# Attention core with 256-token chunks: one chunk of each half worked as two single 128-token tiles

## The chip, the cores and the metric

One core of one Trainium2 chip runs the whole program. The metric is the device time of one execution in microseconds. The kernel before takes 2043.13 us, the median of three runs.

## The reference, cut to what matters

The input is 8 sequences of 1024 tokens with 256 features, fp32. A mixture-of-experts layer, an attention-like layer and a second expert layer follow each other. The change lies in the attention-like layer:

```python
n = _ln(x, ln_g, ln_b)
W1 = _mlp(n, h1_w1, h1_b1, h1_w2, h1_b2)
W2 = _mlp(n, h2_w1, h2_b1, h2_w2, h2_b2)
W3 = jnp.einsum('bzn,bsn->bzs', W1, W2)
W3 = jnp.tril(W3)
t = jnp.einsum('bzs,bsm->bzm', W3, n)
t = _ln(_gelu(t), ln_g, ln_b)
x1 = x + t
out = x + _mlp(_ln(x1, ln_g, ln_b), fm_w1, fm_b1, fm_w2, fm_b2)
```

There is no softmax between the scores and t. So for a token z, the tokens s that lie in earlier blocks can be summed up first: their part of t is W1[z] times the state, the sum of W2[s]^T n[s] over those blocks. Only the scores inside z's own block have to be formed and masked.

## The kernel before, in words

**Tiling.** The 8192 tokens are worked in 16 halves of 512 tokens, two for each sequence. A half is even (j = 0, 2, ...) where it begins a sequence and odd where it ends one. A tile is 128 tokens, a half has four tiles and two chunks of 256 tokens (c = 0 and 1).

**Order.** The order on each engine is written out by hand as positions. A half j > 0 has 24 positions: 8 for each of the three multi-layer networks h1, h2 (of this half) and fm (of the half before). At each position TensorE issues `up` (six matmuls of 512 columns, L2133), then `down` for the position two earlier (L2163 or L2153), and then, at some positions, a piece of the attention core. ScalarE (ACT) makes two gelus of each `up` result (L1430, L1433), VectorE (DVE) subtracts one from the other (`rest`, L1815) so that `down` can work in a high and a low part.

**The core of half j.** Position 18: scores (`score_tiles`, L2209), for each chunk a block of 128 rows of W2 by 256 columns and one of 128 by 128; ACT copies them out (L1465) and GpSimd (POOL) masks the diagonal blocks (L1348). Position 19: W2 is turned (`turn_w2`, L2217) and copied (L1846). Position 20: the state of each chunk (`state_tiles`, L2226), which DVE copies or adds to the one before (`add_state`, L1857 and L1860). Position 21: t (`t_tiles`): scores times n (L2242), and, where there are tokens in earlier chunks, W1 times the state (L2246); ACT takes the gelu of t into `t_rows` (L1470). Position 22: the next half's n is turned (`turn`, L2121). Half 0 has the same pieces in a row at its end, with nothing between them.

**Banks.** All these pieces write the two PSUM banks `work0` and `work1` in turn; who reads a bank must be done before the next piece writes it. `t_rows` is free from position 13, where TensorE has turned it, to position 21, where the gelu of t is written. Each fp32 matmul of the program stands in the trace as two matmul rows; those of the networks, in the rounded form fp32r, as one.

**The queues.** SyncE's and POOL's DMAs are not touched by the change. POOL, in order: roots, gathers and scatters for the neighbouring expert layers, the mask, and three sums over rows (L1336 to L1341) that wait for DVE's L1773.

Of the kernel before, what the change touches and what calls it, by code (L numbers as in the profile page):

```python
# [16 lines left out]
ALU = mybir.AluOpType  # L17
# [859 lines left out]
def attention_to_end(nc, outer, tag, consts, routing, home, w, base_d, y_d, base1_d, xs_d, meta_d, y2_d, out):  # L877
# [21 lines left out]
    TURN_M, TURN_N, SCORES, W2_ROWS, STATE, T_SUM, TURN_X, LOGITS, PLACES = range(9)  # L899
# [8 lines left out]
    for j in range(HALVES + 2):  # L908
# [13 lines left out]
        if j < HALVES:  # L922
            take_work(j, SCORES)
            take_work(j, W2_ROWS, (0, 1) if j % 2 == 0 else (0,))
            take_work(j, STATE, (0, 1) if j % 2 == 0 else (0,))
            take_work(j, T_SUM)
# [3 lines left out]
    def work_use(bank, j, what):  # L930
        return uses[bank, j, what]

    with ExitStack() as ctx:
# [7 lines left out]
        gelu = [sb(f"gelu{s}", [P, GW]) for s in range(GELUS)]  # L941
        hid_pair = [sb(f"hid{s}", [P, 2, GW], fr) for s in range(PARTS)]
        hid = [[pair[:, part, :] for part in range(2)] for pair in hid_pair]
        over_hid = [nc.alloc_sbuf_tensor_at(f"final_total{11 + s}", [P, GT, D], fp32, offset=nc.sbuf_base - 2 * 4 * 2 * GW + s * 4 * 2 * GW) for s in range(2)]
        proj = room[:, 4096:6144].rearrange("p (m k n) -> p m k n", m=2, k=KD)
# [108 lines left out]

        def z_of(j):
            return zn[:, j % 2, 0, :, :]
# [4 lines left out]
        def state_of(j, chunk):  # L1061

            return state[(2 * (j % 2) + chunk) % 2]
# [49 lines left out]
        for j in range(HALVES):  # L1113
            state_count.append(state_count[-1] + (2 if j % 2 == 0 else 1))

        def w2_count(j):

            return state_count[j]
# [131 lines left out]
        def _(pool):  # L1250
# [92 lines left out]
            def mask(j):  # L1343
                for c in range(2):
                    pool.wait_ge(scores_out, 2 * j + c + 1)
                    for lo in (0, CW):
# [69 lines left out]
        def _(act):  # L1416
# [42 lines left out]
            def copy_scores(j):  # L1459
# [174 lines left out]
        def _(dve):  # L1634
# [213 lines left out]
            def add_state(j):  # L1848
                for c in range(2 - j % 2):
                    dve.wait_ge(work_full[c], work_use(c, j, STATE) + 1)  # L1850
                    if j:

                        for bank in range(2):
                            dve.wait_ge(work_full[bank], work_use(bank, j - 1, T_SUM) + 1)
                    dst, src = state_of(j, c), work[c][:, :].rearrange("p (k d) -> p k d", k=KD)
                    if j % 2 == 0 and c == 0:
                        dve.tensor_copy(dst[:, :, :], src).then_inc(state_ready, 1)  # L1857
                    else:
                        dve.wait_ge(state_ready, state_count[j] + c)
                        dve.tensor_tensor(dst[:, :, :], src, state_of(j, c - 1)[:, :, :], ALU.add).then_inc(state_ready, 1)  # L1860

            def iteration(j):
                more, h = j + 1 < HALVES, j - 2
                for pos in range(PER if j else 2 * FC):
# [46 lines left out]
                    if j == 0 and pos == 15:  # L1911
# [3 lines left out]
                        add_state(0)  # L1915
# [4 lines left out]
                    if pos == 20:  # L1920
                        add_state(j)
# [190 lines left out]
        def _(pe):  # L2112
            TERMS = ((0, 0), (1, 0), (0, 1))

            def turn(src, emptied, count):

                for k in range(KD):
                    if emptied is not None:
                        pe.wait_ge(emptied, count + k + 1)
# [100 lines left out]
            def state_tiles(j):  # L2220

                for c in range(2 - j % 2):
                    pe.wait_ge(w2_ready, w2_count(j) + c + 1)
                    for k in range(KD):
                        for s in range(2):
                            last = pe.matmul(work[c][:, k * D:(k + 1) * D], w2_rows[:, 2 * c + s, k * P:(k + 1) * P], n_of(j)[:, 2 * c + s, :], start=(s == 0), stop=(s == 1))  # L2226
                    last.then_inc(work_full[c], 1)

            def t_tiles(j):

                for c in range(2):
                    before = j % 2 or c
                    if j % 2 == 0 or c == 0:

                        pe.wait_ge(state_ready, state_count[j] + c + 1)
                    else:
                        pe.wait_ge(state_ready, state_count[j] + 1)
                    pe.wait_ge(masked, 4 * j + 2 * c + 2)
                    for d in range(2):
                        out = work[c][:, d * D:(d + 1) * D]  # L2240
                        for s in range(d + 1):
                            last = pe.matmul(out, scores[:, c, d * P:(d + 1) * P] if s == 0 else scores[:, c, CW:CW + P], n_of(j)[:, 2 * c + s, :],  # L2242
                                             start=(s == 0), stop=(s == d and not before))
                        if before:
                            for k in range(KD):
                                last = pe.matmul(out, proj[:, 0, k, (2 * c + d) * P:(2 * c + d + 1) * P], state_of(j, c - 1)[:, k, :], start=False, stop=(k == KD - 1))  # L2246
                    last.then_inc(work_full[c], 1)

            def iteration(j):
                positions = PER if j else 2 * FC  # L2250
                for pos in range(positions):
# [9 lines left out]
                    if j:  # L2261
# [4 lines left out]
                        if pos == 13:  # L2266
                            pe.wait_ge(t_step, 16 * j)
                            if j == 1:
                                turn(t_rows, t_gelu, 0)
# [9 lines left out]
                        if pos == 20:  # L2279
                            state_tiles(j)  # L2280
                        if pos == 21:
                            t_tiles(j)
# [245 lines left out]
```

## Time and profile before

| | |
|---|---|
| three runs, median (lowest to highest) | 2043.13 us (2042.89 to 2043.6) |
| profiled execution, first to last instruction (its only time shown) | 2040.7 us |
| TensorE busy | 1945.9 us, 95% of the span |
| VectorE, ScalarE, GpSimd busy | 1305.8, 1093.1, 1102.2 us |
| mean granted TensorE clock | 0.982 of full speed |
| attention halves 0 to 15, from about 396 to 1684 us of the span | positions as above |

The profiled execution's span is 2.4 us under the median of the runs; what lies around it (start and end of the program) is in the runs only. A row of the timeline is the start in us, the duration, the engine, the line, the operation and how many instructions are merged in it; the duration of a merged row goes from its first start to its last end. Matmuls overlap, so a row's duration is longer than the step from one to the next.

### The profile page before, as it was taken

To read this page: it belongs to the slowest core of one execution; us is meant where nothing else is said; L and a number is where in the kernel's file an instruction comes from. 1 tells how busy PE (TensorE), PEld (TensorE's weight loads), DVE (VectorE), ACT (ScalarE), POOL (GpSimd) and SP (SyncE) were. 2 spreads that over 40 slices of the span, in tenths; PEclk is the share of its full clock that TensorE was granted. 3 is DMA by queue.
4 is the path that set the end of the run, shared out by engine and by line. 5 is a ranking of instruction groups with operands and counts; after the bars stand their busy time and mean duration, and the time that the engine had idled before them with its cause. 6 is when DMAs were issued, how large, how long until landed. Compare 5 with 4: busy or idle time off the path is not lost.

```text
span 2040.7 us, 32594 instructions
## 1 busy us (share of the span) xinstructions
PE 1945.9 (95%) x11074; PEld 1661.1 (81%) x11074; DVE 1305.8 (64%) x3481; ACT 1093.1 (54%) x1988; POOL 1102.2 (54%) x1262
## 2 busy tenths in 40 slices
PE   6997999699999999999999999999999996899998
PEld 4776999578888888888888888888888886599975
DVE  5996677456557576575665765756657545466659
ACT  6873777334545455454454544544545534577775
POOL 5664777442364555645546456455552532577753
PEclk9998999899999999999999999999999998899998
DMA  8544999790022032120320311102100040499969
GB/s 278 183 158 135 323 325 323 227 278 22 13 92 83 22 104 60 45 88 16 104 83 22 104 29 34 42 21 62 42 22 24 19 132 9 93 343 328 397 234 333
DMA packets 234295, 267.99 MB, mean 131 GB/s; under 512 B 25425, under 2 KB 184210, under 8 KB 234130
## 3 DMA queue, kind: packets, MB, share of 16 engines
q1 hardware_dynamic: 205458, 198.69, 29.9%
q0 software_dynamic: 28672, 67.22, 9.7%
q8 instruction: 89, 1.46, 0.3%
q14 instruction: 76, 0.62, 0.1%
HBM read 149.31 MB, written 116.52 MB: 130 GB/s over the span
## 4 chain that ended last, share of the span: by engine, by line
PE 67%; DVE 8%; issue 3%; ACT 2%; POOL 1%; DMA 1%; DVEq 0%; SPq 0%; ACTq 0%; POOLq 0%
PE attention_ring L2133 23%; PE attention_acc L2163 14%; PE attention_acc L2153 9%; PE attention_acc L2403 3%; PE attention_ring L2391 2%; PE attention_acc L2391 2%; PE attention_work L2209 2%; DVE attention_hid L1815 2%; PE attention_work L2226 2%; PE attention_work L2242 2%; PE attention_work L2246 2%; PE attention_ring L2378 1%; PE attention_work L2121 1%; PE attention_work L2183 1%; ACT attention_xn L1443 1%
## 5 line engine op out<-in xcount | busy, mean ns | idle before, releaser
L1815 DVE TENSOR_TENSOR attention_hid<-attention_gelu,attention_hid 128x512 fp32r<-128x512 f32 x384 | 286.7, 747 | 487.7 <-ACT attention_gelu L1433 318.2
L1430 ACT ACTIVATE attention_hid<-attention_ring,home_b 128x512 fp32r<-128x512 f32 x384 | 264.3, 688 | 533.7 <-PE attention_ring L2133 533.2
L2163 PE MATMUL attention_acc<-attention_hid,home_w_h 128*128 128x512 f32 x1024 | 361.2, 391 | 3.1 <-DVE home_room L1832 1.7
L1433 ACT ACTIVATE attention_gelu<-attention_ring,home_b 128x512 f32<-128x512 f32 x384 | 261.6, 681 | 0.0
L2163 PEld LDWEIGHTS attention_acc<-attention_hid,home_w_h 128*128 128x128 f32 x1024 | 192.2, 188 | 49.3 <-DVE home_room L1832 9.4
L2133 PE MATMUL attention_ring<-attention_n_t_h,home_w_h 128*128 128x512 f32 x512 | 203.9, 398 | 1.6 <-DVE attention_n_t_l L1807 1.6
L2153 PE MATMUL attention_acc<-home_w_h,attention_hid 128*128 128x256 f32 x1024 | 204.4, 283 | 0.0
L2133 PE MATMUL attention_ring<-attention_n_t_h,home_w_l 128*128 128x512 f32 x512 | 199.8, 390 | 0.0
L2133 PE MATMUL attention_ring<-attention_n_t_l,home_w_h 128*128 128x512 f32 x512 | 199.5, 390 | 0.0
L2163 PE MATMUL attention_acc<-attention_hid,home_w_l 128*128 128x512 f32 x512 | 199.3, 389 | 0.0
L1260 POOL DMA_INDIRECT home_room<-expert_rows,routing_slots x128 | 136.5, 1066 | 91.6 <-DVE home_room L1646 38.1
L1314 POOL DMA_INDIRECT slot_rows<-attention_xn,attention_slot_at x120 | 123.6, 1030 | 94.7 <-DVE attention_meta_at L1750 62.8
L2153 PEld LDWEIGHTS attention_acc<-home_w_h,attention_hid 128*128 128x128 f32 x1024 | 167.6, 190 | 5.0
L684 POOL DMA_INDIRECT early_xg<-xn_rows,routing_affine x124 | 136.1, 1098 | 40.8 <-issue 39.9
L1325 POOL DMA_INDIRECT slot_ids<-attention_row_id,attention_meta_at x128 | 127.4, 995 | 36.9 <-issue 36.9
L2153 PE MATMUL attention_acc<-home_w_l,attention_hid 128*128 128x256 f32 x512 | 144.6, 282 | 0.0
L2133 PE MATMUL attention_ring<-attention_m_t_h,home_w_h 128*128 128x512 f32 x256 | 112.5, 440 | 1.4 <-DVE attention_m_t_l L1807 1.4
L2133 PEld LDWEIGHTS attention_ring<-attention_n_t_l,home_w_h 128*128 128x128 f32 x512 | 96.1, 188 | 20.7
L2163 PEld LDWEIGHTS attention_acc<-attention_hid,home_w_l 128*128 128x128 f32 x512 | 96.1, 188 | 19.5
L2133 PEld LDWEIGHTS attention_ring<-attention_n_t_h,home_w_h 128*128 128x128 f32 x512 | 96.4, 188 | 19.0 <-DVE attention_n_t_l L1807 1.8
L2133 PEld LDWEIGHTS attention_ring<-attention_n_t_h,home_w_l 128*128 128x128 f32 x512 | 96.5, 188 | 16.9
L2133 PE MATMUL attention_ring<-attention_m_t_l,home_w_h 128*128 128x512 f32 x256 | 101.4, 396 | 0.0
(330 smaller groups left out, 4819.3 us busy)
## 6 DMA issues: line engine op xcount, KB each, us to landing
early_w<-in_L_ffn_w SPq DMA_DIRECT2D x64, 256.0 KB, 4.7
expert_rows<-experts_y SPq DMA_DIRECT2D x64, 256.0 KB, 4.0
slot_rows<-const_zeros SPq DMA_DIRECT2D x16, 1024.0 KB, 10.3
token_rows<-const_zeros SPq DMA_DIRECT2D x16, 1024.0 KB, 10.0
home_room<-in_L_ffn_w SPq DMA_DIRECT2D x64, 256.0 KB, 4.8
final_y_rows<-token_rows SPq DMA_DIRECT2D x32, 512.0 KB, 7.7
dispatch_x_in<-in_L_attn_x SPq DMA_DIRECT2D x16, 512.0 KB, 6.7
xn_rows<-dispatch_xn SPq DMA_DIRECT2D x16, 512.0 KB, 4.2
```

What stands on the lines that cost most here:

```text
L684: pool.indirect_dma_start(out=xg[e % R][:, c, :], out_offset=None, in_=xn_d, in_offset=bass.IndirectOffsetOnAxis(ap=routing["lists"][:, e, ...
L1260: pool.indirect_dma_start(out=ye[:, t, k, :], out_offset=None, in_=y_d, in_offset=bass.IndirectOffsetOnAxis(ap=routing["slots"][:, j * GT ...
L1314: pool.indirect_dma_start(out=xs_d, out_offset=bass.IndirectOffsetOnAxis(ap=slot_at[h % 2][:, k, t:t + 1], axis=0), in_=xn_of(h)[:, t, :], ...
L1325: pool.indirect_dma_start(out=meta_d, out_offset=bass.IndirectOffsetOnAxis(ap=meta_at[h % 2][:, k, t:t + 1], axis=0), in_=row_id[h % 2][:, ...
L1430: act.activation(hid[n % PARTS][0][:, :], ring[n % RING][:, :], ACT.Gelu, bias=b1[:, m, c:c + 1])
L1433: act.activation(gelu[n % GELUS][:, :], ring[n % RING][:, :], ACT.Gelu, bias=b1[:, m, c:c + 1]).then_inc(ring_free, 1)
L1815: dve.tensor_tensor(hid[n % PARTS][1][:, :], gelu[n % GELUS][:, :], hid[n % PARTS][0][:, :].bitcast(fp32), ALU.subtract).then_inc(hid_read ...
L2133: last = pe.matmul(ring[n % RING][:, :], w1[m][wp][:, k, c * P:(c + 1) * P], rows_t[xp][:, k, :], start=(q == 0), stop=(q == 2 * len(TERMS ...
L2153: last = pe.matmul(acc[e % 3][:, (t % 2) * D:(t % 2 + 1) * D], hid[s][xp][:, t * P:(t + 1) * P], w2[m][wp][:, c, :], start=(c == 0 and q = ...
L2163: last = pe.matmul(acc[e % 3][:, :], w2[m][wp][:, c, k * P:(k + 1) * P], hid[s][xp][:, :], start=(c == 0 and q == 0), stop=(c == FC - 1 an ...
L2391: last = pe.matmul(ps_gu[e % EF][:, half, :], wt[e % EF][:, k, half * INNER:(half + 1) * INNER], xt[e % EX][:, k, :], start=(n == 0), stop ...
L2403: last = pe.matmul(ps_y[e % EF][:, c, :], e_hidden[e % EF][:, c * P:(c + 1) * P], e_w2[e % WR], start=True, stop=True)
```

## The change

In each half one chunk stays as it was: chunk 0 in even halves, chunk 1 in odd ones (`joined`). The other is worked as two single tiles. For it only the two 128x128 diagonal blocks of the scores are formed, and its second tile takes what precedes it from a state that includes its first tile. So an even half has three states (after tiles 0 and 1, after tile 2, after tile 3) and an odd half forms two new ones (after tile 0, after tile 1). The additional state buffers lie in `t_rows`. In even halves t is formed for chunk 1 first and then for chunk 0, because bank 0 holds the third state until DVE has added it; the gelus of t and the turning at position 22 follow that order. Two buffers, `gelu` and `hid`, change places in SBUF.

```diff
-    TURN_M, TURN_N, SCORES, W2_ROWS, STATE, T_SUM, TURN_X, LOGITS, PLACES = range(9)
+    TURN_M, TURN_N, SCORES, W2_ROWS, STATE, THIRD_STATE, T_SUM, TURN_X, LOGITS, PLACES = range(10)
...
+    def joined(j, pair):
+
+        return pair == j % 2
+
+    def score_blocks(j, pair):
+
+        return ((0, CW, 0), (CW, P, 1)) if joined(j, pair) else ((0, P, 0), (P, P, 1))
...
+        def t_order(j):
+
+            return (1, 0) if j % 2 == 0 else (0, 1)
...
+        early_state, late_state = [t_rows[:, 2 * c:2 * c + 2, :] for c in range(2)]
+
+        def state_after(j, n):
+
+            if j % 2 == 0:
+                return (early_state, state[0], state[1])[n]
+            return (state[0], late_state, state[1])[n]
...
-                    act.activation(scores[:, c, :], work[c][:, 0:CW + P], ACT.Copy).then_inc(scores_out, 1)
+                    wide = CW + P if joined(j, c) else CW
+                    act.activation(scores[:, c, 0:wide], work[c][:, 0:wide], ACT.Copy).then_inc(scores_out, 1)
...
-                for c in range(2):
+                for c in t_order(j):
...
+            def add_state(j, n):
+
+                bank, what = (0, THIRD_STATE) if n == 2 else (n, STATE)
+                dve.wait_ge(work_full[bank], work_use(bank, j, what) + 1)
...
+                dst, src = state_after(j, n), work[bank][:, :].rearrange("p (k d) -> p k d", k=KD)
+                if j % 2 == 0 and n == 0:
+                    dve.tensor_copy(dst[:, :, :], src).then_inc(state_ready, 1)
+                else:
+                    dve.wait_ge(state_ready, state_count[j] + n)
+                    dve.tensor_tensor(dst[:, :, :], src, state_after(j, n - 1)[:, :, :], ALU.add).then_inc(state_ready, 1)
...
                     if pos == 20:
-                        add_state(j)
+                        add_state(j, 0)
+                        add_state(j, 1)
+                    if pos == 21 and j % 2 == 0:
+                        add_state(j, 2)
...
-                    for lo, width, s in ((0, CW, 2 * c), (CW, P, 2 * c + 1)):
+                    for lo, width, s in score_blocks(j, c):
+                        at = (2 * c + s) * P
                         for k in range(KD):
-                            last = pe.matmul(work[c][:, lo:lo + width], proj[:, 1, k, s * P:(s + 1) * P], proj[:, 0, k, 2 * (c + 1) * P - width:2 * (c + 1) * P], start=(k == 0), stop=(k == KD - 1))
+                            last = pe.matmul(work[c][:, lo:lo + width], proj[:, 1, k, at:at + P], proj[:, 0, k, at:at + width], start=(k == 0), stop=(k == KD - 1))
...
+            def state_tiles(j, n):
+
+                if j % 2 == 0:
+                    bank, tiles, copied = ((0, (0, 1), 1), (1, (2,), 2), (0, (3,), 2))[n]
+                else:
+                    bank, tiles, copied = ((0, (0,), 1), (1, (1,), 1))[n]
+                pe.wait_ge(w2_ready, w2_count(j) + copied)
+                if n == 2:
+                    pe.wait_ge(state_ready, state_count[j] + 1)
+                if j % 2 and n == 1:
+                    pe.wait_ge(scores_out, 2 * j + 2)
+                for k in range(KD):
+                    for s in tiles:
+                        last = pe.matmul(work[bank][:, k * D:(k + 1) * D], w2_rows[:, s, k * P:(k + 1) * P], n_of(j)[:, s, :], start=(s == tiles[0]), stop=(s == tiles[-1]))
+                last.then_inc(work_full[bank], 1)
...
+                    if j % 2 == 0:
+                        pe.wait_ge(state_ready, state_count[j] + (2 if c else 3))
+                    else:
                         pe.wait_ge(state_ready, state_count[j] + c + 1)
...
+                        t, out = 2 * c + d, work[c][:, d * D:(d + 1) * D]
+                        if joined(j, c):
+                            seen = None if j % 2 == 0 else state_after(j, 1)
+                            parts = [(scores[:, c, d * P:(d + 1) * P], 2 * c)] + ([(scores[:, c, CW:CW + P], 2 * c + 1)] if d else [])
+                        else:
+                            seen = state_after(j, d) if c else state_after(j, d - 1)
+                            parts = [(scores[:, c, d * P:(d + 1) * P], t)]
...
                         if pos == 20:
-                            state_tiles(j)
+                            state_tiles(j, 0)
+                            state_tiles(j, 1)
                         if pos == 21:
+                            if j % 2 == 0:
+                                state_tiles(j, 2)
                             t_tiles(j)
                         if pos == 22 and j + 1 < HALVES:
                             pe.wait_ge(n_ready, 8 * (j + 2))
-                            turn(n_of(j + 1), t_gelu, 2 * j)
+                            turn(n_of(j + 1), t_gelu, 2 * j, t_order(j))
```

How this stands on the engines. TensorE, half 2 (an even one), position 18, the scores. Before:

```order
L2153 MATMUL attention_acc<-home_w_2_h,attention_hid 128x256
L2209 MATMUL attention_work<-home_room 128x256 x2
L2209 MATMUL attention_work<-home_room 128x128 x2
L2209 MATMUL attention_work<-home_room 128x256 x2
L2209 MATMUL attention_work<-home_room 128x128 x2
L2133 MATMUL attention_ring<-attention_m_t_h,home_w_2_h 128x512
```

Now:

```order
L2177 MATMUL attention_acc<-home_w_2_l,attention_hid 128x256
L2177 MATMUL attention_acc<-home_w_2_h,attention_hid 128x256
L2234 MATMUL attention_work<-home_room 128x256 x2
L2234 MATMUL attention_work<-home_room 128x128 x6
L2157 MATMUL attention_ring<-attention_m_t_h,home_w_2_h 128x512
```

Two matmuls of 256 columns have become two of 128; nothing else has moved there.

TensorE, half 2, position 21: the t block (L2242 scores times n, L2246 W1 times a state; now L2278 and L2281). Before:

```order
L2153 MATMUL attention_acc<-home_w_2_h,attention_hid 128x256
L2242 MATMUL attention_work<-home_room,attention_scores 128x256 x4
L2246 MATMUL attention_work<-attention_state,home_room 128x256 x2
L2242 MATMUL attention_work<-home_room,attention_scores 128x256 x2
L2246 MATMUL attention_work<-attention_state,home_room 128x256 x2
L2133 MATMUL attention_ring<-attention_m_t_h,home_w_2_h 128x512
```

Now, where L2258 is the third state's matmuls:

```order
L2177 MATMUL attention_acc<-home_w_2_h,attention_hid 128x256
L2258 MATMUL attention_work<-home_room,attention_w_rows 128x256 x2
L2278 MATMUL attention_work<-home_room,attention_scores 128x256
L2281 MATMUL attention_work<-attention_t_rows,home_room 128x256 x2
L2278 MATMUL attention_work<-home_room,attention_scores 128x256
L2281 MATMUL attention_work<-attention_state,home_room 128x256 x2
L2278 MATMUL attention_work<-home_room,attention_scores 128x256 x3
L2157 MATMUL attention_ring<-attention_m_t_h,home_w_2_h 128x512
```

Two state matmuls have come here from position 20, and the t block has nine matmuls where it had ten.

VectorE, half 2, positions 20 to 22 (`hid` is `rest`, `home_room` at L1773 the next half's n). Before:

```order
L1815 TENSOR_TENSOR attention_hid0<-attention_gelu0,attention_hid0 128x512
L1773 SCALAR_TENSOR_TENSOR home_room<-home_room,attention_x_root,home_b_row 128x256 x4
L1857 COPY attention_state0<-attention_work0 128x512
L1860 TENSOR_TENSOR attention_state1<-attention_work1,attention_state0 128x512
L1815 TENSOR_TENSOR attention_hid1<-attention_gelu1,attention_hid1 128x512
L1815 TENSOR_TENSOR attention_hid2<-attention_gelu0,attention_hid2 128x512
```

Now:

```order
L1834 TENSOR_TENSOR attention_hid0<-attention_gelu0,attention_hid0 128x512
L1792 SCALAR_TENSOR_TENSOR home_room<-home_room,attention_x_root,home_b_row 128x256 x4
L1877 COPY attention_t_rows<-attention_work0 128x512
L1880 TENSOR_TENSOR attention_state0<-attention_work1,attention_t_rows 128x512
L1834 TENSOR_TENSOR attention_hid1<-attention_gelu1,attention_hid1 128x512
L1880 TENSOR_TENSOR attention_state1<-attention_work0,attention_state0 128x512
L1834 TENSOR_TENSOR attention_hid2<-attention_gelu0,attention_hid2 128x512
```

One addition is new, between two `rest` operations; in an odd half the new one stands at position 20, right behind the first.

## Rows read from the trace of the kernel before

**Rows 1.** Busy time of each engine in one window, halves 1 to 15.

```profile
core 0: us, PE busy (x) PEld busy (x) DVE busy (x) ACT busy (x) POOL busy (x), PEclk, DMA share, GB/s
452.40:1679.20 1226.80, 1224.99 (x6544) 1053.98 (x6543) 758.94 (x2064) 585.61 (x976) 623.19 (x719) 1.00 0.17 54
```

**Rows 2.** Waits of TensorE over the span: us in total, times, longest.

```profile
PE attention_work L2121 <- DVE attention_t_rows L1802: 12.9, 1, 12.9
...
PE attention_acc L2163 <- DVE home_room L1832: 1.7, 2, 1.3
...
PE attention_ring L2133 <- DVE attention_n_t_l L1807: 1.6, 1, 1.6
```

**Rows 3.** Timeline of TensorE, half 6 (even), positions 18 to 20.

```profile
917.58 2.78 PE L2209 MATMUL attention_work<-home_room 128*128 128x256 f32 x16
920.12 0.47 PE L2133 MATMUL attention_ring<-attention_m_t_h,home_w_h 128*128 128x512 f32 x1
...
926.70 3.62 PE L2226 MATMUL attention_work<-home_room,attention_w_rows 128*128 128x256 f32 x16
929.97 0.58 PE L2133 MATMUL attention_ring<-attention_m_t_h,home_w_h 128*128 128x512 f32 x1
```

**Rows 4.** By line: durations in ns, min/median/max, first and last start, forms.

```profile
L2209 PEld LDWEIGHTS attention_work<-home_room x256: 186/190/192, 443.2 to 1662.0; 128*128 128x128 f32 x128
L2209 PE MATMUL attention_work<-home_room x256: 272/326/454, 443.3 to 1662.2; 128*128 128x256 f32 x64, 128*128 128x128 f32 x64
...
L2246 PE MATMUL attention_work<-attention_state,home_room x192: 379/379/379, 452.6 to 1678.7; 128*128 128x256 f32 x192
```

**Rows 5.** Timeline of TensorE, the router's matmuls of 64 columns at the end.

```profile
1715.83 1.90 PE L2183 MATMUL attention_work<-home_gate,attention_w_rows 128*128 128x64 f32 x16
```

**Rows 6.** Timeline of TensorE, half 6, positions 21 and 22.

```profile
932.98 1.89 PE L2242 MATMUL attention_work<-home_room,attention_scores 128*128 128x256 f32 x8
934.70 1.03 PE L2246 MATMUL attention_work<-attention_state,home_room 128*128 128x256 f32 x4
935.57 1.03 PE L2242 MATMUL attention_work<-home_room,attention_scores 128*128 128x256 f32 x4
936.43 1.03 PE L2246 MATMUL attention_work<-attention_state,home_room 128*128 128x256 f32 x4
937.11 0.58 PE L2133 MATMUL attention_ring<-attention_m_t_h,home_w_h 128*128 128x512 f32 x1
```

**Rows 7.** Timeline of VectorE, half 6, positions 20 and 21.

```profile
929.03 0.68 DVE L1857 COPY attention_state<-attention_work 128x512 f32<-128x512 f32 x1
930.35 0.69 DVE L1860 TENSOR_TENSOR attention_state<-attention_work,attention_state 128x512 f32<-128x512 f32 x1 [0.64 <-PE attention_work L2226]
933.11 0.95 DVE L1815 TENSOR_TENSOR attention_hid<-attention_gelu,attention_hid 128x512 fp32r<-128x512 f32 x1 [2.06 <-ACT attention_gelu L1433]
```

**Rows 8.** Timeline of VectorE and TensorE, half 7 (odd), positions 20 and 21.

```profile
1011.27 0.68 DVE L1860 TENSOR_TENSOR attention_state<-attention_work,attention_state 128x512 f32<-128x512 f32 x1
1013.63 1.16 DVE L1815 TENSOR_TENSOR attention_hid<-attention_gelu,attention_hid 128x512 fp32r<-128x512 f32 x1 [1.67 <-ACT attention_gelu L1433]
...
1016.52 0.59 PE L2242 MATMUL attention_work<-home_room,attention_scores 128*128 128x256 f32 x2
```

**Rows 9.** Timeline around the turning of n, end of half 6: VectorE, TensorE.

```profile
941.38 1.29 DVE L1807 TENSOR_TENSOR attention_n_t_l<-attention_work,attention_n_t_h 128x512 fp32r<-128x512 f32 x2 [0.44 <-ACT attention_n_t_h L1422]
...
943.82 0.40 PE L2133 MATMUL attention_ring<-attention_n_t_h,home_w_h 128*128 128x512 f32 x1
```

**Rows 10.** Timeline of GpSimd, from half 6 to half 7.

```profile
947.18 1.14 POOL L1325 DMA_INDIRECT slot_ids<-attention_row_id,attention_meta_at  x1 [0.30 <-issue]
949.16 0.23 POOL L1268 TENSOR_SCALAR attention_small<-attention_u_mv 128x4 f32<-128x4 f32 x1 [0.85 <-DVE attention_u_mv L1653]
```

**Rows 11.** Timeline of half 0's end: TensorE, VectorE, ScalarE's copies of the scores.

```profile
445.97 1.40 PE L2217 MATMUL attention_work<-const_eye,home_room 128*128 128x128 f32 x8
447.35 3.72 PE L2226 MATMUL attention_work<-home_room,attention_w_rows 128*128 128x256 f32 x16
...
449.38 0.69 DVE L1857 COPY attention_state<-attention_work 128x512 f32<-128x512 f32 x1 [1.29 <-PE attention_work L2226]
...
446.17 0.49 ACT L1465 ACTIVATE attention_scores<-attention_work 128x384 f32<-128x384 f32 x1 [0.82 <-PE attention_work L2209]
...
455.43 0.60 ACT L1470 ACTIVATE attention_t_rows<-attention_work 128x512 f32<-128x512 f32 x1 [2.42 <-PE attention_work L2246]
```

More of the change, by code:

```diff
@@ L944, in attention_to_end @@
         over_hid = [nc.alloc_sbuf_tensor_at(f"final_total{11 + s}", [P, GT, D], fp32, offset=nc.sbuf_base - 2 * 4 * 2 * GW + s * 4 * 2 * GW) for s in range(2)]
+        gelu = [sb(f"gelu{s}", [P, GW]) for s in range(GELUS)]
         proj = room[:, 4096:6144].rearrange("p (m k n) -> p m k n", m=2, k=KD)
@@ L1846, in copy_w2_rows @@
                     dve.tensor_copy(w2_rows[:, 2 * c:2 * c + 2, :], work[c][:, :].rearrange("p (t d) -> p t d", t=2)).then_inc(w2_ready, 1)
[L1848 to L1860, printed above, removed]
+            def add_state(j, n):
+                bank, what = (0, THIRD_STATE) if n == 2 else (n, STATE)
+                dve.wait_ge(work_full[bank], work_use(bank, j, what) + 1)
+                if j and n == 0:
+                    for c in range(2):
+                        dve.wait_ge(work_full[c], work_use(c, j - 1, T_SUM) + 1)
+                dst, src = state_after(j, n), work[bank][:, :].rearrange("p (k d) -> p k d", k=KD)
[4 more added lines that the diff above has]
+                    dve.tensor_tensor(dst[:, :, :], src, state_after(j, n - 1)[:, :, :], ALU.add).then_inc(state_ready, 1)
             def iteration(j):
@@ L1914, in iteration @@
                         copy_w2_rows(0)
-                        add_state(0)
+                        for n in range(3):
+                            add_state(0, n)
                     if pos == 17:
@@ L2113, in _, with turn @@
             TERMS = ((0, 0), (1, 0), (0, 1))
-            def turn(src, emptied, count):
-                for k in range(KD):
+            def turn(src, emptied, count, order=(0, 1)):
+                for n, k in enumerate(order):
                     if emptied is not None:
-                        pe.wait_ge(emptied, count + k + 1)
+                        pe.wait_ge(emptied, count + n + 1)
                     for t in range(GT):
@@ L2218, in turn_w2 @@
                     last.then_inc(work_full[c], 1)
[L2220 to L2227, printed above, removed]
+            def state_tiles(j, n):
[12 more added lines that the diff above has]
+                last.then_inc(work_full[bank], 1)
@@ L2238, in t_tiles @@
                     pe.wait_ge(masked, 4 * j + 2 * c + 2)
                     for d in range(2):
[L2240 to L2244, printed above, removed]
+                        t, out = 2 * c + d, work[c][:, d * D:(d + 1) * D]
@@ new lines, in t_tiles @@
+                        if joined(j, c):
[4 more added lines that the diff above has]
+                            parts = [(scores[:, c, d * P:(d + 1) * P], t)]
+                        for n, (weights, s) in enumerate(parts):
+                            last = pe.matmul(out, weights, n_of(j)[:, s, :], start=(n == 0), stop=(seen is None and n == len(parts) - 1))
@@ L2245, in t_tiles @@
+                        if seen is not None:
                             for k in range(KD):
-                                last = pe.matmul(out, proj[:, 0, k, (2 * c + d) * P:(2 * c + d + 1) * P], state_of(j, c - 1)[:, k, :], start=False, stop=(k == KD - 1))
+                                last = pe.matmul(out, proj[:, 0, k, t * P:(t + 1) * P], seen[:, k, :], start=False, stop=(k == KD - 1))
                     last.then_inc(work_full[c], 1)
@@ L2292, in iteration @@
                     turn_w2(0)
-                    state_tiles(0)
+                    for n in range(3):
+                        state_tiles(0, n)
                     t_tiles(0)
```

21 lines of the change are left out of this document (8 added, 13 removed).

## The prediction, made before the changed kernel ran

> **What bounds the kernel now.** I read the busy times by stretch first. From the end of half 0 to the t block of half 15 [rows 1] TensorE is busy for 1224.99 of 1226.80 us at a granted clock of 1.00; VectorE has 758.94, ScalarE 585.61 and GpSimd 623.19 us in the same stretch. The waits of TensorE say the same from the other side [rows 2]: over the whole span its one long wait is 12.9 us for the last t rows, behind half 15, and the others that touch this stretch are of 1.3 and 1.6 us, once each. So in the attention halves the time is the length of TensorE's stream of instructions. What shortens that stream shortens the program, as long as no other engine becomes late; what is added to VectorE costs nothing while its results come in time.
>
> **What a matmul of this core costs.** In half 6 the state's 16 matmul rows of 256 columns last 3.62 us from the first start to the last end [rows 3]. The last alone lasts 0.38, as every row of 256 columns at the neighbouring line L2246 does [rows 4], so one step is (3.62 - 0.38) / 15 = 0.216 us. The scores are 8 rows of 256 and 8 of 128 columns, 2.78 us, and the last, a narrow one, takes about 0.27 [rows 3, 4]. That leaves 2.51 us: 8 steps of 0.216 and 7 narrow ones of (2.51 - 1.73) / 7 = 0.111 us. Each fp32 matmul of the program is two such rows.
>
> **Part 1, the scores.** Two matmuls of 256 columns become two of 128, in every half: 4 rows by (0.216 - 0.111) = 0.42 us. In other cases a narrow matmul could stop getting cheaper because its weights still have to be loaded. The router's rows of 64 columns show where that floor is: 16 of them last 1.90 us [rows 5], which is (1.90 - 0.22) / 15 = 0.112 a step. 64 columns cost what 128 cost, so 128 columns stand just on the floor, and the halving from 256 to 128 is still had in full.
>
> The Trainium skill, page "TensorE: Matmul & The Clock Gate", section "Back-to-back issue gap", speaks against this term: in a stream of weight loads and matmuls it gives about 81 ns per matmul at 128 columns and 131 ns at 512, a saving far from proportional. Put on a line, that makes 128 columns cost 0.83 of 256, an estimate from that page: 4 x 0.037 = 0.15 us for this part and 2033.9 us for the whole, where the row gives 0.42. The figures are not for fp32 matmuls of two rows, and the trace has the narrow step itself at 0.111. I take the row.
>
> **Part 2, the t block.** The split chunk gives up the off-diagonal block of its scores and takes its first tile through the state, which its second tile needs anyway. One matmul of 256 columns goes in every half: in an even half the block has 9 matmuls where it had 10, in an odd one 13 where it had 14. Two rows, 0.43 us. I look at the even block before [rows 6]: 20 rows from 932.98 to the next `up` at 937.11.
>
> **Part 3, the state matmuls** are as many as before: 8 in an even half, 4 in an odd one, all of 256 columns. In even halves two of them move from position 20 to the head of the t block; they stand beside fp32 matmuls at both places, so no change between the two kinds of matmul is added. Zero.
>
> **Part 4, VectorE.** One more addition per half. The present one takes 0.69 us [rows 7]; 16 of them are 11 us on an engine that is idle for 468 of the 1226.80 us [rows 1]. It is hidden if three results still come in time. I lay out half 6 with the new stream. The first `up` after the state starts at 929.97 before and, with 12 rows instead of 16, at 929.1. The two networks' pieces up to the t block take 932.98 - 929.97 = 3.0 us, so the third state's matmuls start at 932.1 and end at 933.0 (the shift of 0.42 by the scores moves all engines alike and is left out).
> - They overwrite bank 0 and wait for the copy of the first state, done at 929.7 [rows 7]: 2.4 us in hand.
> - Chunk 1 of t needs the second state: addition done at about 930.4, needed at 933.0.
> - Chunk 0 of t needs bank 0 back, which is the new addition. On VectorE it is queued behind the `rest` of position 21, which waits for a gelu and began at 933.11 [rows 7]; now it begins 0.86 earlier, is done by about 933.1 even at its present 0.95 us, and the addition ends at about 933.9. TensorE spends 12 rows, 2.6 us, on chunk 1 of t and asks at 935.6. 1.7 us in hand. This is why the order is turned round.
>
> What is queued behind the new addition on VectorE is the `rest` of position 22, which before began 6 us later. In an odd half both additions stand at position 20: the first ends at 1011.95 and VectorE then waits 1.67 us for the next gelu [rows 8]; the second fits in with 1.0 us left, and chunk 1 of t asks for it only at 1016.5. Zero for all of it.
>
> **Part 5, the turned order at position 22** of an even half. Bank 1 is turned first, and ScalarE, which begins with bank 0, starts four narrow rows later, 0.44 us. VectorE's low part follows it and ended at 942.67, while TensorE asked at 943.82 [rows 9]: of 1.15 us, 0.7 are left. Zero.
>
> **Part 6, GpSimd.** Its mask has as many blocks as before. Its chain from the sums to the next roots is not shortened, while TensorE's is, by the 0.43 of the t block. GpSimd had 0.85 us of idle time there [rows 10] and keeps 0.4. Zero.
>
> **Part 7, half 0,** where nothing stands between the pieces. The third state's matmuls wait for the first copy. The state's matmuls start at 447.35, the first 12 rows end at 449.94, the copy ends at 450.07 [rows 11] and a signal takes about 0.1: a wait of 0.2 us. Against it the copy of chunk 1's scores, on which the turning of W2 waited there (8 rows that last 1.40 instead of 1.04 us), has 256 instead of 384 columns: 0.49 us before; the 512-column copy takes 0.60 [rows 11], so about 0.11 less. Together +0.1.
>
> **Part 8, what no row prices.** `gelu` and `hid` change places; no row shows that an address matters. Both are written and read by engines with idle time in these halves. From below, zero; from above, if VectorE's `rest` were to run at its slowest of rows 7 and 8 (1.16 instead of 0.7 us) all the time, 0.5 us a position, inside the 2.06 and 1.67 us that it was idle before the same operation there. Zero, for the range and the sum.
>
> **The sum.** 16 x (0.42 + 0.43) = 13.6 us, less 0.1: 13.5 us. Behind the halves nothing changes in length: the 12.9 us wait [rows 2] starts and ends with the last `rest`, so it moves as a whole, and with it the pause after which the clock is lower. The profiled span goes from 2040.7 to 2027.2 us, and the median of the runs, 2.4 us above the span, from 2043.1 to **2029.6 us**, 0.66% less.
>
> **The rivals.**
> - **A, part is given back.** Small waits appear in the overlapped halves (GpSimd's 0.4 us or the 0.7 us of part 5 are spent in some of them), or the expert stage behind, whose transfers have their own phase, does not take the whole shift. For it: both margins shrink. Against it: both end in other engines' idle time. 0.1 to 0.25 us in each of 15 halves is 1.5 to 4 us back: 2031 to 2033.6 us.
> - **B, narrow matmuls don't halve.** The matmul before a weight load may have to cover it: a load's row lasts 190 ns [rows 4]. If more narrow matmuls in a row, six program matmuls where two stood together, had to wait for their weights in full, a step would be 0.19 and a half would gain 4 x 0.026 + 0.43 = 0.53 us, together 8.5 less 0.1: 2034.7 us. The narrow steps and the router's 16 in a row speak against it. The Trainium skill's spacing rule quoted above points the same way.
> - **C, slower: the third state's addition holds up chunk 0 of t.** It happens in the 8 even halves if VectorE comes to it late, for the price of the lateness beyond 1.7 us. To undo 13.5 us and add 4.1 it would have to end 1.7 + 2.2 = 3.9 us later than laid out, in each of them; at 3.0 to 3.9 us late the result is within 0.2%. Against it: VectorE waits 2.06 us for the gelu just before [rows 7], so it is not late. The time would be over 2047 us.
>
> **How the numbers follow.** Forecast 0.85 (2028.4 to 2031.0 us: the 0.216 and 0.111 steps are each good to 0.002, some 0.3 us over the halves, and the runs spread by 0.7), A 0.08, B 0.03, C slower 0.02, C within 0.2% 0.02. A measurement of this kernel can tell about 0.2%, 4.1 us, from no change. The forecast, A and B are all faster by more than that: faster 0.96, within 0.2% 0.02, slower 0.02. The range of 2028.0 to 2032.6 holds the forecast with room on both sides for the unpriced and most of A.
>
> **What would show it.** Right: the stretch between the t blocks of two neighbouring halves is shorter by 0.85 us; the scores' 16 rows take 0.42 us less; TensorE's busy share in the halves stays above 99.8%; no wait of TensorE for the state's addition except one of about 0.2 us in half 0. Wrong: waits of L2258 or L2278 for VectorE in the even halves (C), scores rows whose narrow step is above 0.15 us (B), waits of `up` for the low part of n at a half's start or longer tail stages (A), or gaps in TensorE's stream that no wait explains.

## The result, and the profile after

The changed kernel takes 2029.38 us, the median of five runs (2027.46 to 2030.95), where the kernel before took 2043.13 in the same series (2042.18 to 2043.6). The ratio is 0.993 with a 95% interval of 0.992 to 0.994. The profiled span went from 2040.7 to 2027.0 us. The forecast was 2029.6 us and a span of 2027.2.

The busy times of the changed kernel between the same two events as in [rows 1], from 1.5 us behind the start of half 0's t block to the end of the last row of half 15's t block:

```profile
core 0: us, PE busy (x) PEld busy (x) DVE busy (x) ACT busy (x) POOL busy (x), PEclk, DMA share, GB/s
452.10:1665.90 1213.80, 1212.03 (x6512) 1043.11 (x6511) 769.68 (x2079) 583.53 (x976) 618.80 (x719) 1.00 0.17 55
```

The window is 13.0 us shorter, and TensorE's busy time with it (1224.99 to 1212.03 us). VectorE has 10.7 us more (758.94 to 769.68), about the 16 additions of 0.68 to 0.69 us; it shows nowhere in the time.

TensorE's timeline in half 6, to set beside [rows 3, 6]: the scores, then the state and the t block.

```profile
912.32 2.36 PE L2234 MATMUL attention_work<-home_room 128*128 128x256 f32 x16
914.44 0.48 PE L2157 MATMUL attention_ring<-attention_m_t_h,home_w_h 128*128 128x512 f32 x1
...
921.02 2.75 PE L2258 MATMUL attention_work<-home_room,attention_w_rows 128*128 128x256 f32 x12
926.43 1.03 PE L2258 MATMUL attention_work<-home_room,attention_w_rows 128*128 128x256 f32 x4
927.30 0.59 PE L2278 MATMUL attention_work<-home_room,attention_scores 128*128 128x256 f32 x2
927.73 1.03 PE L2281 MATMUL attention_work<-attention_t_rows,home_room 128*128 128x256 f32 x4
928.59 0.59 PE L2278 MATMUL attention_work<-home_room,attention_scores 128*128 128x256 f32 x2
929.02 1.03 PE L2281 MATMUL attention_work<-attention_state,home_room 128*128 128x256 f32 x4
929.89 1.46 PE L2278 MATMUL attention_work<-home_room,attention_scores 128*128 128x256 f32 x6
```

The 16 rows of the scores last 2.36 us where they lasted 2.78: 0.42 less. The t block is 18 rows, one behind the other with 0.215 us a step and no "idle before" entry. The last row shown, at 929.89, is the t of chunk 0, the one that waits for the third addition. VectorE had ended that addition (the last line below, 927.62 + 0.68 = 928.30) 1.59 us earlier:

```profile
924.14 0.69 DVE L1880 TENSOR_TENSOR attention_state<-attention_work,attention_t_rows 128x512 f32<-128x512 f32 x1
926.58 1.12 DVE L1834 TENSOR_TENSOR attention_hid<-attention_gelu,attention_hid 128x512 fp32r<-128x512 f32 x1 [1.75 <-ACT attention_gelu L1451]
927.62 0.68 DVE L1880 TENSOR_TENSOR attention_state<-attention_work,attention_state 128x512 f32<-128x512 f32 x1
```

In what follows one length is compared, since it leaves out the stages that the change doesn't touch: **the attention stretch**, from the start of the first scores row (half 0) to the start of the last row of t (half 15). It is read from the rows by line, which give the first and last start; of before they are 443.3 (scores) and 1678.7 (t) [rows 4], of the changed kernel:

```profile
L2234 PE MATMUL attention_work<-home_room x256: 271/275/454, 443.1 to 1649.3; 128*128 128x128 f32 x96, 128*128 128x256 f32 x32
...
L2281 PE MATMUL attention_work<-attention_t_rows,home_room x96: 379/379/380, 451.0 to 1665.4; 128*128 128x256 f32 x96
```

That is 1235.4 us before and 1222.3 now, 13.1 less. From the t block of half 6 to that of half 7 it takes 79.67 us where it took 80.52 (starts at 927.30 and 1006.97, before at 932.98 and 1013.50): 0.85 less in one half. In the row for the scores the numbers of the shapes tell the edit: 96 narrow and 32 wide rows, where [rows 4] have 64 and 64 of each (the counts of the shapes add up to half of the 256 rows).

### The profile page after: what moved, and what is told of

Its sections match the earlier page's. It is cut to its first block, busy times and chain, and to the rows that moved or that the text cites. A ratio compares the mean times of both kernels' runs of the same rounds, so it can differ in the third digit from the quotient of the medians.

```text
span 2027.0 us, 32571 instructions
## 1 busy us (share of the span) xinstructions
PE 1931.6 (95%) x11042; PEld 1650.7 (81%) x11042; DVE 1318.9 (65%) x3497; ACT 1090.5 (54%) x1988; POOL 1099.5 (54%) x1262
## 4 chain that ended last, share of the span: by engine, by line
PE 66%; DVE 9%; issue 3%; ACT 2%; POOL 1%; DMA 1%; DVEq 0%; SPq 0%; ACTq 0%; POOLq 0%
PE attention_ring L2157 22%; PE attention_acc L2187 14%; PE attention_acc L2177 9%; PE attention_acc L2442 3%; PE attention_ring L2430 2%; DVE attention_hid L1834 2%; PE attention_acc L2430 2%; PE attention_work L2258 2%; PE attention_work L2281 2%; PE attention_work L2234 2%; PE attention_work L2278 2%; PE attention_work L2207 1%; PE attention_ring L2417 1%; PE attention_work L2145 1%; ACT attention_xn L1461 1%
## 5 line engine op out<-in xcount | busy, mean ns | idle before, releaser
L2177 PEld LDWEIGHTS attention_acc<-home_w_l,attention_hid 128*128 128x128 f32 x512 | 97.2, 190 | 5.1
```

Of the source, the lines that this page charges most:

```text
L2177: last = pe.matmul(acc[e % 3][:, (t % 2) * D:(t % 2 + 1) * D], hid[s][xp][:, t * P:(t + 1) * P], w2[m][wp][:, c, :], start=(c == 0 and q = ...
```

## The experiments

Eight kernels ran, four in each of two series, beside the kernel before (medians 2044.9 and 2043.58 us there). All but one start from the changed kernel.

| kernel | attention stretch, us | against the changed kernel | profiled span | median of runs |
|---|---|---|---|---|
| before | 1235.4 | +13.1 | 2040.7 | 2043.13 |
| changed | 1222.3 | | 2027.0 | 2029.38 |
| scores wide again | 1229.0 | +6.7 | 2037.7 | 2038.2 |
| before, scores narrow only | 1229.1 | +6.8 | 2036.2 | 2038.52 |
| chunk 0 of t first | 1231.3 | +9.0 | 2038.4 | 2040.17 |
| gelu and hid in old places | 1222.3 | 0.0 | 2028.6 | 2030.41 |
| third addition 2 copies later | 1222.2 | -0.1 | 2029.2 | 2030.89 |
| 3 copies later | 1227.5 | +5.2 | 2032.3 | 2036.22 |
| 5 copies later | 1245.7 | +23.4 | 2055.5 | 2057.59 |
| narrow blocks of 64 columns | 1222.2 | -0.1 | 2029.5 | 2032.86 |

Outside the stretch the profiles differ by up to 5 us (span less stretch is 804.7 to 809.8 us), also between kernels that are the same there, so single spans and medians carry that much noise. The stretch is the same to 0.1 us in the four kernels for which it should be (1222.2 and 1222.3), each read from one profile.

This matters for the expectations that follow. Six of them name a span of the whole program, and all six came out longer than expected: by 1.6 to 4.0 us, and with five copies by 7.5. They were reckoned from the spans of the two main kernels (2027.0 and, for the scores alone, 2040.7 us), and the changed kernel has the shortest time outside the stretch of all ten profiles, 804.7 us. What is concluded below therefore rests on the stretch.

**The two parts apart.** First the scores' part is undone:

```diff
-        return ((0, CW, 0), (CW, P, 1)) if joined(j, pair) else ((0, P, 0), (P, P, 1))
+        return ((0, CW, 0), (CW, P, 1)) if joined(j, pair) else ((0, CW, 0), (P, P, 1))
```

> The changed kernel with the scores' term undone: in the split chunk the first block is again formed 256 columns wide (its second half is then overwritten by the other diagonal block), everything else as in the changed kernel. My theory, TensorE's row steps add up: 4 rows per half cost 0.216 instead of 0.111 us, so 16 x 0.42 = 6.7 us more than the changed kernel, span 2033.7 us and runs at about 2036.1. Rival (narrow matmuls bring little, the gain is in the t block or elsewhere): within 1 us of the changed kernel's 2027.0 us span.

Then it is done alone, in the kernel before:

```diff
-                    for lo, width, s in ((0, CW, 2 * c), (CW, P, 2 * c + 1)):
+                    for lo, width, s in ((0, CW if c == j % 2 else P, 2 * c), (CW, P, 2 * c + 1)):
                         for k in range(KD):
-                            last = pe.matmul(work[c][:, lo:lo + width], proj[:, 1, k, s * P:(s + 1) * P], proj[:, 0, k, 2 * (c + 1) * P - width:2 * (c + 1) * P], start=(k == 0), stop=(k == KD - 1))
+                            last = pe.matmul(work[c][:, lo:lo + width], proj[:, 1, k, s * P:(s + 1) * P], proj[:, 0, k, s * P:s * P + width], start=(k == 0), stop=(k == KD - 1))
```

> The kernel before with only the scores' term done: in one chunk of each half the first block of scores is formed 128 columns wide; the off-diagonal block, which this kernel's t block still multiplies, is left out of the computation and holds old values. Theory of added steps: 16 x 0.42 = 6.7 us less than before, span 2034.0 us. Rival that the two parts only pay together (for instance that the gain comes from the shifted positions): less than 3 us.

Undone, the scores cost 6.7 us in the stretch (6.7 expected); the 16 rows of half 6 last 2.78 us again:

```profile
916.48 2.78 PE L2234 MATMUL attention_work<-home_room 128*128 128x256 f32 x16
919.02 0.48 PE L2157 MATMUL attention_ring<-attention_m_t_h,home_w_h 128*128 128x512 f32 x1
```

Alone, in the kernel before, they bring 1235.4 - 1229.1 = 6.3 us, and the t part, put on top of them, 6.8. In the other order the t part alone brings 1235.4 - 1229.0 = 6.4 us and the scores on top of it 6.7. Either way the sum is 13.1, as it must be between the same two kernels; what the two orders test is that each part brings nearly the same alone (6.3, 6.4) and on top of the other (6.7, 6.8). The rival of the expectation, that they pay only together, is out. The 0.4 us that they bring more together than apart no run explains.

**The order of the t block.** Chunk 0 first in even halves, with the first state moved so that this stays free of races:

```diff
-            return (1, 0) if j % 2 == 0 else (0, 1)
+            return (0, 1)
...
-                return (early_state, state[0], state[1])[n]
+                return (late_state, state[0], state[1])[n]
...
-                        pe.wait_ge(state_ready, state_count[j] + (2 if c else 3))
+                        pe.wait_ge(state_ready, state_count[j] + 3)
```

> The changed kernel with the order of the t block, of its gelus and of the turning in even halves set back to chunk 0, then chunk 1; the first state of an even half lies in the upper half of the t rows instead of the lower, so that this order is free of races. Theory: chunk 0 of t asks for bank 0 right behind the third state's matmuls, about 927.3 us in half 6, while VectorE's third addition ended at 928.3 and signals about 0.1 later: a wait of 1.0 to 1.1 us in each of the 7 overlapped even halves and 0.5 to 1.0 us in half 0, together 8 us, span about 2035 us; a wait of TensorE's scores-times-n line for the state's addition shows, 8 times. Rival (TensorE's queue or the other engines' idle time swallow it, the order doesn't matter): within 1 us of 2027.0 us.

The wait came, eight times, as TensorE's waits over the span tell (us in total, times, longest):

```profile
PE attention_work L2278 <- DVE attention_state L1880: 7.0, 8, 0.9
```

and in half 6 it stands in front of the first row of the t block (TensorE), with the addition that releases it (VectorE):

```profile
930.38 1.03 PE L2258 MATMUL attention_work<-home_room,attention_w_rows 128*128 128x256 f32 x4
932.30 1.99 PE L2278 MATMUL attention_work<-home_room,attention_scores 128*128 128x256 f32 x8 [0.89 <-DVE attention_state L1880]
...
931.57 0.68 DVE L1880 TENSOR_TENSOR attention_state<-attention_work,attention_state 128x512 f32<-128x512 f32 x1
```

The addition ends at 932.25 and the matmul starts at 932.30, so a signal takes 0.05 us. The start-to-start step from the last state group to the t block is 932.30 - 930.38 = 1.92 us where the changed kernel has 0.87 (926.43 to 927.30): 1.05 us for an idle entry of 0.89, because the entry counts only from the modelled end of the last matmul (931.41). The t block behind the wait takes 0.11 us more as well, from its first row to the next `up`: 3.80 us (932.30 to 936.10) where the changed kernel has 3.69 (927.30 to 930.99). Eight times about 1.15 is near the 9.0 us of the stretch; 8 were expected. Two thirds of the change's gain would be gone in this order. It is part of the design and no detail.

**The places in SBUF.** `gelu` allocated ahead of `hid` again:

> The changed kernel with the gelu and hid buffers in their old places in SBUF. Theory: addresses have no price, span within 0.7 us of 2027.0 us, VectorE's rest operation at the same mean of 749 ns. Rival (the exchange of places is worth part of the gain): 1 us or more slower, and another mean for that operation.

The stretch is the same to 0.1 us, and VectorE's `rest` has a mean of 750 ns against 749. In the stretch the exchange has no price. The span is 1.6 us longer, more than the 0.7 that the expectation allowed and as its rival asked for; but the 1.6 lie outside the stretch, where profiles differ by up to 5 us, and the other sign of the rival, another mean of `rest`, is missing.

**The margin behind the third addition, measured.** Two, three or five copies of bank 0 are put on VectorE ahead of it; this is the edit for five:

```diff
+        idled = sem("idled")
...
+                if n == 2:
+                    for i in range(5):
+                        if i:
+                            dve.wait_ge(idled, 5 * (j // 2) + i)
+                        dve.tensor_copy(dst[:, :, :], src).then_inc(idled, 1)
+                    dve.wait_ge(idled, 5 * (j // 2 + 1))
```

> The changed kernel with two extra copies of bank 0 on VectorE ahead of the third state's addition in each even half (each waits for the one before, 0.79 us from start to start as the first copy and the second addition stand in half 6). Theory: the addition ended at 928.30 and TensorE asked at 929.89; less about 0.05 for the signal that is 1.54 us in hand. Two copies are 1.58 us late: 0.04 us of wait in each of 8 even halves, 0.3 us in all, span within 1 us of the changed kernel (attention stretch 1222.3 us). Rival (VectorE's added work isn't free in these halves): two to three of these operations in 8 halves, 12 us of work, cost several us.

> The same with three extra copies, 2.37 us late. Theory: 2.37 - 1.54 = 0.83 us of wait in each of 8 even halves, 6.6 us, attention stretch 1229 us. If the margin were used up elsewhere first, more; if TensorE's wait began later, less.

> The same with five extra copies, 3.95 us late. This is the prediction's rival C made true: 3.95 - 1.54 = 2.41 us in each of 8 even halves, 19.3 us, attention stretch 1241.6 us and span 2046 to 2048 us, so slower than the kernel before; a wait of TensorE's scores-times-n line for the state's addition, 8 times, 2.2 to 2.4 us each. A different slope than one for one beyond the margin would speak against added waits.

A copy is cheaper than I had taken, 0.72 us from start to start instead of 0.79, as VectorE's timeline with three of them shows:

```profile
928.90 2.13 DVE L1881 COPY attention_state<-attention_work 128x512 f32<-128x512 f32 x3
931.06 0.69 DVE L1887 TENSOR_TENSOR attention_state<-attention_work,attention_state 128x512 f32<-128x512 f32 x1
```

So the additions come about 1.44, 2.16 (931.06 - 928.90) and 3.6 us late with two, three and five copies. With two copies nothing is lost in the stretch, although VectorE does 12 us more work. With three, TensorE's t block waits: its row for chunk 0,

```profile
930.30 1.03 PE L2288 MATMUL attention_work<-attention_state,home_room 128*128 128x256 f32 x4
931.81 1.56 PE L2285 MATMUL attention_work<-home_room,attention_scores 128*128 128x256 f32 x6 [0.48 <-DVE attention_state L1887]
```

starts 1.51 us after the group before it instead of 0.87 (929.02 to 929.89), 0.64 us late, and over the eight even halves the stretch is 5.2 us longer, 0.65 a half. The margin is thus 2.16 - 0.65 = 1.5 us: the 1.59 of the rows less the signal. Expected were 6.6 us; the price of a copy was the miss, not the margin. From there every microsecond of lateness costs one, in each even half: with five copies the lateness is 3.6 us, the waits cost 2.1 us a half, and the time 2057.59 us, 14 us slower than the kernel before (ratio 1.0065, 1.0047 to 1.0082). That is the prediction's rival C, made true by force: the mechanism exists, and the changed kernel stands 1.5 us away from it. Its price is higher than the prediction had put it (see the next section).

But the stretch grew by 23.4 us where 19.3 were expected, and only 8 x 2.1 = 17 of them are waits. The other 6 are told in the last section.

**How narrow a block can get.** The diagonal blocks of 128 columns are cut to 64:

```diff
                     for lo, width, s in score_blocks(j, c):
                         at = (2 * c + s) * P
+                        width = width if width == CW else P // 2
```

> The changed kernel with every narrow block of scores formed only 64 instead of 128 columns wide; the other 64 columns of these blocks are left out of the computation and hold old values. 12 of the 16 rows of a half's scores become half as wide. Theory from the router's rows (64 columns, 0.112 us a step): nothing is gained, the step stays at 0.109 to 0.112 us because the weights have to be loaded, the scores' 16 rows still take 2.12 us, attention stretch 1222 us. Rival (a row costs its columns): 12 x 0.055 = 0.66 us less per half, 10.6 us in all.

Half the columns of 12 rows are gone, and nothing is gained: the stretch is 1222.2 us, and from the first row of the scores to the next `up` it is 2.12 us in half 6, as it is with 128 columns (912.32 to 914.44).

```profile
913.28 2.31 PE L2235 MATMUL attention_work<-home_room 128*128 128x256 f32 x16
915.40 0.48 PE L2157 MATMUL attention_ring<-attention_m_t_h,home_w_h 128*128 128x512 f32 x1
```

So 128 columns are on the floor of about 0.11 us a row, as the router's rows had said [rows 5]. The Trainium skill, page "TensorE: Matmul & The Clock Gate", section "LDWEIGHTS (loading the stationary operand)", gives the time of a weight load in ns as its columns divided by 1.2; for 128 columns that makes 107 ns, an estimate from that page. The floor of about 0.11 us a row here agrees with it. That the load of the weights is what sets the floor is argued and not shown: no run narrowed the blocks with the weights kept. The profile's own duration for such a load, 190 ns [rows 4], is not its price in this stream.

## Why the prediction was right, point by point

- **What bounds the kernel.** TensorE's stream, at 99.85% of the stretch [rows 1]. What was taken out of it came out of the stretch nearly one for one in three kernels (changed, scores only, and the t part with wide scores: 13.1, 6.3 and 6.4 us of 13.6, 6.7 and 6.9), and what was added to VectorE (some 23 us with two copies: 11 of additions and 12 of copies) cost nothing there while its result was in time. One reading was wrong without harm: over the whole span the 12.9 us wait is not TensorE's only long one. Four others of 8.4 to 14.1 us, the longest of them below, stand ahead of the stretch, and so do the waits of 1.3 and 1.6 us; from half 1 on the stretch of the kernel before has a single wait, of 0.4 us.

```profile
PE attention_acc L74 <- DVE home_room L1931: 14.1, 1, 14.1
```

- **Parts 1 and 2, scores and t.** 0.42 and 0.43 us per half were forecast. Measured: 2.78 to 2.36 us for the scores; two rows of 0.215 for t. In the stretch 6.3 to 6.7 and 6.4 to 6.8 us, where 16 times the steps are 6.7 and 6.9.
- **The spacing figures of the Trainium skill** (page "TensorE: Matmul & The Clock Gate", section "Back-to-back issue gap"), weighed against part 1, would have given 0.15 us there and 2033.9 us, both estimates; measured were 0.42 us in half 6 and 2029.4. The narrow step of the trace was the right guide, and the figures don't carry over to these fp32 matmuls of two rows. Rival B (weights to be waited for in full) would have shown as narrow steps of 0.19 us; with up to twelve narrow rows behind each other they stayed at 0.11.
- **Part 4, VectorE.** Forecast: the third addition ends 1.7 us before TensorE asks. Measured: 1.59, mostly because `rest` took 1.12 us there and not 0.95. The copy experiments give 1.5 usable. The claim that the turned order is what hides it held with 9.0 us.
- **Part 5, the turned order at position 22.** VectorE's low part ended at 937.00 and the next `up` started at 937.71: 0.7 us in hand, as forecast.

```profile
935.71 1.29 DVE L1826 TENSOR_TENSOR attention_n_t_l<-attention_work,attention_n_t_h 128x512 fp32r<-128x512 f32 x2 [0.88 <-ACT attention_n_t_h L1440]
...
937.71 0.40 PE L2157 MATMUL attention_ring<-attention_n_t_h,home_w_h 128*128 128x512 f32 x1
```

- **Part 6, GpSimd.** Its idle time before the next roots is 0.58 us, where 0.4 was expected to be left of 0.85:

```profile
943.05 0.23 POOL L1286 TENSOR_SCALAR attention_small<-attention_u_mv 128x4 f32<-128x4 f32 x1 [0.58 <-DVE attention_u_mv L1672]
```

- **Part 7, half 0.** Off by a little: a loss of 0.1 was forecast, 0.25 was measured. The state block there went from 3.56 us (447.35 to 450.91, where t began) to 3.81, so the wait for the first copy cost 0.25 and not 0.2; and the narrower copy of the scores, put at 0.11, saved nothing: the turning of W2 took 1.38 us from its start to that of the state as before. The first line is of the kernel before, the others of the changed one.

```profile
450.91 1.89 PE L2242 MATMUL attention_work<-home_room,attention_scores 128*128 128x256 f32 x8
...
445.41 1.29 PE L2242 MATMUL attention_work<-const_eye,home_room 128*128 128x128 f32 x8
446.79 3.97 PE L2258 MATMUL attention_work<-home_room,attention_w_rows 128*128 128x256 f32 x16
450.60 0.59 PE L2278 MATMUL attention_work<-home_room,attention_scores 128*128 128x256 f32 x2
```

- **Part 8, the places in SBUF:** no price in the stretch, as forecast.
- **Rival A** did not come: the only wait of TensorE between half 1 and half 15 is one of 0.3 us, where it was 0.4 before. The wait behind half 15 moved as a whole (12.9 us before, 13.0 now).

```profile
PE attention_work L2145 <- DVE attention_t_rows L1821: 13.0, 1, 13.0
```

- **Rival C** did not come, but its price was wrong. The prediction put an addition 3.0 to 3.9 us late within 0.2% of the kernel before. With five copies it was 3.6 us late and the kernel 0.65% slower. Beyond the margin, 3.6 - 1.7 = 1.9 us in eight halves would be 15 us; the span grew by 28.5: 17 of waits, some 6 of a lower clock in the stretch, and 5 outside it that are not explained.

The sum came to 13.6 less 0.1; the stretch shows 13.1 and the span 13.7. The 0.6 between them is inside what the stages around the stretch vary by, so the near-exact median is in part luck. The mechanism doesn't hang on that: it is shown by the stretch, part by part.

## What to carry to other kernels

Where one engine is busy for 99.8% of a stretch, a change to its stream can be priced by start-to-start steps of its own rows, taken apart by shape, and the total is then good to a few per cent. The work is to show for every other engine that it still answers in time, in microseconds in hand at the exact instruction that waits; an order that looks arbitrary (here chunk 1 before chunk 0) can hold most of the gain. And before matmuls are cut narrower, look for a row of a still narrower shape: it shows the floor below which nothing more is won.

## What the runs showed of the hardware

With five copies, the eight waits in the t block were alike (idle entries of 1.93 us, 1.82 in half 0), but in halves 8, 10, 12 and 14 TensorE came out of them at a lower granted clock. The windows of halves 6 and 8 around the wait (the columns as above, TensorE alone):

```profile
core 0: us, PE busy (x), PEclk, DMA share, GB/s
936.00:946.00 10.00, 8.07 (x48) 1.00 0.02 2
...
1104.40:1107.00 2.60, 2.50 (x7) 0.59 0.01 0
```

and the same six rows of t in both, after the same idle entry:

```profile
939.13 1.56 PE L2285 MATMUL attention_work<-home_room,attention_scores 128*128 128x256 f32 x6 [1.93 <-DVE attention_state L1887]
...
1104.50 2.59 PE L2285 MATMUL attention_work<-home_room,attention_scores 128*128 128x256 f32 x6 [1.93 <-DVE attention_state L1887]
```

In half 8 a stretch is run at the lower of the two levels, 1.2 instead of 2.4 GHz, which the row at 0.59 mixes with a little of the higher. From the t block of half 8 to that of half 9 it then takes 83.5 us, where it took 81.8 from half 6 to half 7. Halves 10 and 12 lose 1.6 us as well and half 14 about 1.3; together that makes the 6 us of the 23.4 that are not waits. What made the same wait harmless in halves 0 to 6 and costly in 8 to 14 no run here tells apart. With three copies (idle entries of 0.5 us) and with chunk 0 first (0.9 us) the clock reads 1.00 over the whole stretch. So a wait added in this stream has in some halves cost more than itself; a price per wait taken from the shorter ones was too low for the longer.
